# Cross-attention and ternary feed-forward on one core: the stores of keys and values issued from ScalarE's queue

## The reference, cut to what matters

```python
x = x + xattn(layernorm(x), ctx, ctx)      # x: 4 x 2048 x 512, ctx: 4 x 154 x 512
x = x + ffn(layernorm(x))

def xattn(q, k, v):                        # 16 heads of 32, 8 of keys and values
    q1, q2 = split(q @ Wq.T); k1, k2 = split(k @ Wk.T); v = v @ Wv.T
    w = softmax(q1 k1) - lam * softmax(q2 k2)
    return (rmsnorm(w @ v) * g * 0.2...) @ Wo.T

def ffn(x):
    scale = 1 / mean(abs(w))               # one for w1 (2048 x 512), one for w2
    wq = clip(round(w * scale), -1, 1) / scale
    h = gelu(layernorm(x) @ wq1.T + b1)
    return layernorm(h) @ wq2.T + b2
```

## Time and profile before

| | |
|---|---|
| median of 3 runs | 2423.88 us (2423.76 to 2427.24) |
| the profiled execution | 2423.49 us, its span 2421.5 us |
| PE busy | 2286.6 us, 94% |
| DVE, ACT, POOL busy | 71%, 55%, 41% |
| mean granted clock of PE | 0.983 |
| the prologue, until the first scores (PE L1344) | 163.5 us |

### The profile page before, as it was taken

How to read it: one execution, slowest core, us unless ns; L and a number is a source line. 1 busy time by engine, 2 the same in 40 slices (tenths; PEclk the granted TensorE clock), 3 DMA queues, 4 the chain that set the end, 5 groups by cost and what they waited for, 6 DMA issues and landing times.

```text
span 2421.5 us, 35774 instructions
## 1 busy us (share of the span) xinstructions
PE 2286.6 (94%) x13791; PEld 1083.1 (45%) x13791; DVE 1714.2 (71%) x2701; ACT 1339.7 (55%) x1945; POOL 993.4 (41%) x807
## 2 busy tenths in 40 slices
PE   8679999999999999999989999999999999999978
PEld 5344534445353544535344454534445453544433
DVE  4677768686785868678676867868676786867663
ACT  3435655556465555656555555655556565555544
POOL 0102625436172534627153452715346271534517
PEclk9779999999999999999999999999999999999989
DMA  7412103030210303021130302112040211203000
GB/s 262 120 25 62 27 24 83 15 92 15 78 30 29 78 15 92 15 66 27 43 79 15 92 15 66 28 47 59 15 107 15 66 28 50 56 15 75 15 22 18
DMA packets 105661, 125.88 MB, mean 52 GB/s; under 512 B 22512, under 2 KB 74284, under 8 KB 104980
## 3 DMA queue, kind: packets, MB, share of 16 engines
q1 hardware_dynamic: 105492, 123.60, 18.4%
HBM read 51.80 MB, written 20.36 MB: 30 GB/s over the span
## 4 chain that ended last, share of the span: by engine, by line
PE 70%; DVE 17%; DMA 3%; ACT 3%; POOL 3%; issue 3%; SPq 1%; POOLq 0%; ACTq 0%; DVEq 0%
PE ps L1421 16%; PE ps L1443 9%; PE ps L1433 9%; PE ps L1319 5%; PE ps L1366 5%; PE ps L1344 4%; PE ps L1264 4%; PE ps L1373 4%; PE ps L1265 3%; PE ps L1266 3%; DVE attn_raw L993 2%; DVE arena L1052 2%; DVE arena L941 2%; DMA arena<-in_x 2%; DVE arena L955 2%
## 5 line engine op out<-in xcount | busy, mean ns | idle before, releaser
L563 POOL TENSOR_TENSOR attn_raw<-attn_raw 128x512 f32<-128x512 f32 x448 | 579.1, 1311 | 153.5 <-ACT attn_raw L720 146.2
L1421 PE MATMUL ps<-rows,w1T 128*128 128x512 f16 x2048 | 486.9, 381 | 24.8 <-DVE rows L1047 24.8
L955 DVE TENSOR_REDUCE arena<-ps 128x3 f32<-128x462 f32 (+1 forms) x704 | 413.0, 618 | 111.0 <-PE ps L1319 110.1
L529 POOL TENSOR_TENSOR q<-q 128x512 f16<-128x512 f32 x128 | 158.3, 1241 | 723.3 <-ACT q L666 706.6
L715 ACT ACTIVATE attn_raw<-ps,vec_cols,wstep 128x512 f32<-128x512 f32 x256 | 198.7, 776 | 276.3 <-PE ps L1421 274.4
L1052 DVE SCALAR_TENSOR_TENSOR arena<-attn_raw,vec_cols,arena 128x512 f16<-128x512 f32 x256 | 231.8, 905 | 86.1 <-ACT arena L718 84.5
L1421 PEld LDWEIGHTS ps<-rows,w1T 128*128 128x128 f16 x2048 | 191.8, 98 | 222.1 <-DVE rows L1047 38.0
L1443 PE MATMUL ps<-w2T,arena 128*128 128x512 f16 x1088 | 271.2, 379 | 0.0
L686 ACT ACTIVATE arena<-ps 128x1024 f32<-128x1024 f32 x128 | 131.6, 1028 | 228.3 <-PE ps L1344 228.3
L975 DVE SCALAR_TENSOR_TENSOR p<-arena,p 128x512 f16<-128x512 f32 x128 | 88.1, 688 | 236.7 <-ACT p L690 236.7
L1319 PE MATMUL ps<-k_att,stack_raw 96*128 96x154 f16 x2048 | 222.0, 233 | 27.2 <-DVE arena L955 25.2
(11 more groups left out here) (183 smaller groups left out, 3478.7 us busy)
## 6 DMA issues: line engine op xcount, KB each, us to landing
stack_raw<-q SPq DMA_DIRECT2D x768, 64.0 KB, 2.0
arena<-in_x SPq DMA_DIRECT2D x64, 256.0 KB, 2.7
out<-arena SPq DMA_DIRECT2D x64, 256.0 KB, 2.1
arena<-in_x SPq DMA_DIRECT2D x15, 1024.0 KB, 6.2
arena<-in_L_ffn_w SPq DMA_DIRECT2D x7, 1024.0 KB, 10.1
stack_raw<-in_L_xattn_Wq SPq DMA_DIRECT2D x8, 256.0 KB, 5.8
k_att<-k_store SPq DMA_DIRECT2D x4, 490.0 KB
k_store<-attn_raw SPq DMA_DIRECT2D x12, 160.0 KB
```

Of the source, the lines that this page charges most:

```text
L563: ins = pool.tensor_tensor(acc[:, e, :], acc[:, e, :], src[:, j % NG, :], ALU.add)
L955: dve.tensor_reduce(negmax[:, tt, u0:u1], ps[:, row_bank(c, tb), 0:(u1 - u0) * S].rearrange("p (u s) -> p u s", s=S), AX.X, ALU.max, negat ...
L1421: ins = pe.matmul(ps[:, B_H + j % 2, :], w1T[:, k, j * P:(j + 1) * P], rows16[:, e, k, :], start=(k == 0 and e == 0), stop=(k == KD - 1 an ...
```

## The change

ACT issues the stores, each right behind the work of a tile: constant rows at tile 12, keys of m at tile 13 + m, values of b at tile 18 + b. The buffers of values 2 and 3 stand in `q32` and in half of `q16`; both are cleared at the start, and the memset and the wait ahead of batch 2 are gone. The first queries' copies wait for these two stores instead. Each value store has a semaphore of its own. The sums of pieces 6, 7 and 8 stand beside tiles 23, 24 and 25. The transposes of block 1 (x1) stand behind m7 on PE and behind m8 on DVE, ahead of the bias vector.

```diff
-                     "m6 t15 m7 m8 m9 m10 b0 x1 n0")
+                     "m6 t15 m7 x1 m8 m9 m10 b0 n0")
...
-DVE_PROLOGUE = tokens("x0 a0 ... m6 m7 m8 m9 m10 n0 b0 x1 n1")
+DVE_PROLOGUE = tokens("x0 a0 ... m6 m7 m8 x1 m9 m10 n0 b0 n1")
-ACT_PROLOGUE = tokens("x0 q0 q1 a0 q2 t0 t1 ...
+ACT_PROLOGUE = tokens("x0 q0 q1 q2 t0 t1 ...
...
-SUMS_BY_ACT, SUMS_BY_DVE = {17: 0, 19: 2, 20: 4, 22: 5, JH * 2: 7}, {18: 1, 20: 3, JH * 2: 6, JH * 2 + 1: 8}
+SUMS_BY_ACT, SUMS_BY_DVE = {17: 0, 19: 2, 20: 4, 22: 5, 24: 7}, {18: 1, 20: 3, 23: 6, 25: 8}
...
-        v_new = [attn_raw[:, at:at + 3 * TB // 2] for at in (6 * TB, 15 * TB // 2, 0, 3 * TB // 2)]
-        v_first, v_second = attn_raw[:, 6 * TB:], attn_raw[:, 0:3 * TB]
+        v_first = attn_raw[:, 6 * TB:]
+        v_new = [v_first[:, 0:3 * TB // 2], v_first[:, 3 * TB // 2:],
+                 q32[:].rearrange("p b t -> p (b t)")[:, 0:3 * TB // 2],
+                 q16[:, 1].rearrange("p a b t -> p (a b t)").bitcast(F32)[:, 0:3 * TB // 2]]
...
@@ block.sync, setup @@
-                    if n == N_KV_TILES:
-                        sp.wait_ge(s_krows, 2)
-                        for b in range(BATCH):
-                            sp.dma_start(k_store[STK:STKM, :, b, :], krows).then_inc(s_krst, 16)
-                    if 0 <= n - T_KEYS - NSTG < KUNITS // UPT:
-                        store_keys(n - T_KEYS - NSTG)
-                    b = n - T_VALUES - NSTG
-                    if 0 <= b < BATCH:
-                        sp.wait_ge(s_vnew, 9 * b + 9)
-                        sp.dma_start(v_store[b], v_new[b]).then_inc(s_vst[b % 2], 16)
...
@@ block.scalar, setup, at the end of a tile's work @@
+                    if n == T_KEYS:
+                        act.wait_ge(s_krows, 2)
+                        for b in range(BATCH):
+                            act.dma_start(k_store[STK:STKM, :, b, :], krows).then_inc(s_krst, 16)
+                    if 0 <= n - T_KEYS - 1 < KUNITS // UPT:
+                        store_keys(n - T_KEYS - 1)
+                    if 0 <= n - T_VALUES - 2 < BATCH:
+                        store_values(n - T_VALUES - 2)
                     if n in SUMS_BY_ACT:
                         weight_sum(n)
...
@@ block.scalar, q_hi @@
+                if c == 0 and n in (0, 2):
+                    act.wait_ge(s_vst[2 + n // 2], 16)
...
@@ block.vector @@
+                dve.memset(v_new[2], 0.0)
+                dve.memset(v_new[3], 0.0)
                 dve.memset(v_first, 0.0).then_inc(s_v0, 1)
...
-                        if b == 2:
-                            dve.wait_ge(s_kst, 16 * 3 * KUNITS // UPT)
-                            dve.memset(v_second, 0.0).then_inc(s_v0, 1)
-                            dve.wait_ge(s_v0, 2)
```

More of the change, by code:

```diff
@@ L79 @@
 PE_PROLOGUE = tokens("x0 q0 q1 a0 q2 t0 t1 t2 q3 t3 t4 t5 q4 t6 t7 m0 q5 t8 t9 m1 q6 t10 m2 t11 q7 m3 t12 m4 t13 m5 t14 "
-                     "m6 t15 m7 m8 m9 m10 b0 x1 n0")
-DVE_PROLOGUE = tokens("x0 a0 t0 t1 t2 t3 t4 t5 t6 t7 t8 m0 t9 t10 m1 t11 m2 t12 m3 t13 m4 t14 s1 m5 t15 r1 m6 m7 m8 m9 m10 "
-                      "n0 b0 x1 n1")
-ACT_PROLOGUE = tokens("x0 q0 q1 a0 q2 t0 t1 t2 q3 t3 t4 t5 q4 t6 t7 q5 t8 t9 q6 t10 t11 q7 t12 t13 t14 t15 x1")
+                     "m6 t15 m7 x1 m8 m9 m10 b0 n0")
+DVE_PROLOGUE = tokens("x0 a0 t0 t1 t2 t3 t4 t5 t6 t7 t8 m0 t9 t10 m1 t11 m2 t12 m3 t13 m4 t14 s1 m5 t15 r1 m6 m7 m8 x1 m9 m10 "
+                      "n0 b0 n1")
+ACT_PROLOGUE = tokens("x0 q0 q1 q2 t0 t1 t2 q3 t3 t4 t5 q4 t6 t7 q5 t8 t9 q6 t10 t11 q7 t12 t13 t14 t15 x1")
 POOL_PROLOGUE = tokens("q0 q1 q2 q3 q4 q5 q6 s1 q7")
@@ L273, in build @@
         s_kv, s_k_hi, s_k_lo = sem("kv_product"), sem("k_hi"), sem("k_lo")
-        s_kst, s_vst = sem("k_stored"), [sem("v_stored0"), sem("v_stored1")]
+        s_kst, s_vst = sem("k_stored"), [sem(f"v_stored{b}") for b in range(BATCH)]
         s_krst, s_vnew = sem("key_rows_stored"), sem("v_new")
@@ L376, in _ @@
         def _(sp):
[L377 to L383, removed]
             def setup():
@@ L399, in setup @@
                         sp.dma_start(dst, src).then_inc(s_w[piece], 16)
-                    if n == N_KV_TILES:
-                        sp.wait_ge(s_krows, 2)
-                        for b in range(BATCH):
-                            sp.dma_start(k_store[STK:STKM, :, b, :], krows).then_inc(s_krst, 16)
-                    if 0 <= n - T_KEYS - NSTG < KUNITS // UPT:
-                        store_keys(n - T_KEYS - NSTG)
-                    b = n - T_VALUES - NSTG
-                    if 0 <= b < BATCH:
-                        sp.wait_ge(s_vnew, 9 * b + 9)
-                        sp.dma_start(v_store[b], v_new[b]).then_inc(s_vst[b % 2], 16)
                 sp.wait_ge(s_krst, 16 * BATCH)
                 sp.wait_ge(s_kst, 16 * 3 * KUNITS // UPT)
-                for half in range(2):
-                    sp.wait_ge(s_vst[half], 16 * BATCH // 2)
+                for b in range(BATCH):
+                    sp.wait_ge(s_vst[b], 16)
                 load_keys(0)
@@ L605, in _, with store_keys, store_values @@
         def _(act):
+            def store_keys(m):
+                act.wait_ge(s_k_lo, 2 * m + 2)
+                for c3, e in enumerate((0, 0, 1)):
+                    dst = k_store[DH * c3:DH * c3 + DH, UPT * m:UPT * m + UPT, :, :]
+                    act.dma_start(dst.rearrange("d u b s -> u d (b s)"), k16[:, m, e, :, :].rearrange(
+                        "p b s -> p (b s)")).then_inc(s_kst, 16)
+            def store_values(b):
+                act.wait_ge(s_vnew, 9 * b + 9)
+                act.dma_start(v_store[b], v_new[b]).then_inc(s_vst[b], 16)
             def setup():
@@ L645, in weight_sum @@
                 abs_out = q16[:, 0].rearrange("p a b t -> p (a b t)")[:, 0:words]
-                if n not in range(len(tiles)):
-                    act.wait_ge(s_kst, 16 * 3 * KUNITS // UPT)
-                    abs_out = attn_raw[:, 4 * TB:6 * TB].bitcast(F16)
                 act.activation(abs_out, src, ACT.Abs, accum_out=wabs[:, w, col:col + 1]).then_inc(s_aabs, 1)
@@ L761, in _ @@
                     ternary_copy(n)
-                elif what == "a":
-                    weight_sum(JH * 2)
                 elif what == "x":
@@ L855, in weight_scales @@
             def weight_scales():
-                for n in (JH * 2, JH * 2 + 1):
-                    weight_sum(n)
                 dve.tensor_copy(b1ln16[:, :, 0], b1ln_col).then_inc(s_b1ln, 1)
@@ L883, in ternary @@
                 pair = sign_pair(n)
-                if n in (2, 4):
+                if n == 2:
                     for half in range(2):
-                        dve.wait_ge(s_vst[half], 16 * (n // 2))
+                        dve.wait_ge(s_vst[half], 16)
                 if 8 <= n < JH:
@@ L1236, in bias_vector @@
                 pe.wait_ge(s_ternC, JH)
-                wait(pe, s_q32, 0, QM, QM)
+                pe.wait_ge(s_xt_lo, 2 * TT)
                 pe.wait_ge(s_b1ln, 2)
@@ L1525, in _ @@
                     if n:
-                        pe.wait_ge(s_bias, 2)
+                        pe.wait_ge(s_ternC, JH)
+                        wait(pe, s_q32, 0, QM, QM)
                     x_transposes(n)
```

## The result

| | before | changed |
|---|---|---|
| median of 12 runs each, side by side | 2424.78 us (2420.71 to 2428.84) | 2429.53 us (2424.19 to 2433.77) |
| ratio | | 1.0018, 95% interval 1.001 to 1.0026 |
| span of the profiled execution, granted clock | 2421.5 us, 0.983 | 2427.8 us, 0.979 |
| T, `woT_lo` of tile 16 begins | 42.39 | 59.09 |
| X, x0 ready | 87.2 | 94.3 |

The change is 4.75 us slower by the medians, 0.18 to 0.2%. That is small, but the interval lies above 1. The page's first line answers to the earlier trace rows; only PE's busy time has grown, by 4.9 us for the same number of matmuls, with a mean granted clock of 0.979 in place of 0.983.

The account below looks back on a forecast made before the run. With PE 94% busy and the loop untouched, the prologue before the first scores was taken to decide: -8.0 (start included), -4.5 and +0.4 make -12.1, plus 13.1 for ACT's queue gives +1.0 on 2423.49: 2424.5 us, range 2411 to 2430.

Parts of the forecast that it names:

- the case that I called likeliest: Prologue: ACT's queue pays back what the prologue gains; 2421 to 2428 us, chance 0.43.
- the slower rival: Prologue: a cold PE behind a late ACT, T 57 or later; 2428.9 to 2431 us, chance 0.22.
- The start: Start of the kernel: two added memsets ahead of DVE's release of the constants, +1.4 us.
- T to X without the wait: Prologue, tile 16's `woT_lo` to x0 ready: 35.3 us instead of 44.8, wait and memset gone, two sums added.
- The stores on ACT's queue: Prologue: key stores hold ACT about as they held SyncE, T 13.1 us late at 56.9; +13.
- X to m0: Prologue, x0 ready to m0: totals no longer wait for sums and PE keeps its clock; -4.5 us.
- x1: Late prologue: m8 2.0 us later, DVE 2.7 more ahead of m9, 4.3 saved before the maxima's copy; +0.4.
- quick stores: ACT's queue: ACT gets its stores away quickly, T below 51; 2411.4 to 2414.3 us, chance 0.35.
- Cold PE: Prologue: T 57 or later, PE at 1.2 GHz makes values 3 late by 4.4 us; 2428.9 to 2431, chance 0.22.

Follow-up runs that it names:

- e7: Changed kernel with the two added memsets (values 2 and 3) on GpSimd instead of DVE: 2426.91 us, ratio 1.0008 to the kernel before.
- e1: Changed kernel with the key store laid out so that a store leads with 128 rows instead of 4 x 32: 2412.37 us, ratio 0.9961 to the kernel before.
- e14: Changed kernel with all stores issued by GpSimd, block 0's rstd behind the second group: 2413.06 us, ratio 0.9958 to the kernel before.
- e5: Changed kernel with block 1's transposes alone put back behind the bias vector: 2428.61 us, ratio 1.0018 to the kernel before.
- e2: Kernel before with the 128-row layout of the key store, all stores on SyncE's queue: 2411.26 us, ratio 0.9954 to the kernel before.
- e11: As e10, but GpSimd takes the last eighth of the first queries ahead of block 1's rstd: 2411.91 us, ratio 0.9947 to the kernel before.
- e10: As e2, with only the sums of pieces 6, 7 and 8 moved as in the change: 2411.10 us, ratio 0.9945 to the kernel before.
- e3: Changed kernel with all stores back in SyncE's queue, old 4 x 32 layout: 2418.87 us, ratio 0.9984 to the kernel before.
- e16: Changed kernel with 128-row layout, added memsets on GpSimd, block 1's rstd late, stores issued by GpSimd: 2410.23 us, ratio 0.9941 to the kernel before.
- e17: Changed kernel with 128-row layout, added memsets on GpSimd, block 1's rstd late, stores issued by SyncE: 2412.09 us, ratio 0.9949 to the kernel before.
- e4: Kernel before with only the key stores and constant rows moved to ACT's queue: 2427.12 us, ratio 1.0013 to the kernel before.
- e12: Changed kernel with 128-row layout, added memsets on GpSimd, block 1's rstd late, stores on ACT: 2412.59 us, ratio 0.9955 to the kernel before.

## Why the prediction was right, and where its steps were off

The forecast was no change, +1.0, with a range of 2411 to 2430. The measured median, 2429.53, lies inside it by 0.5 us. It is outside the 2421 to 2428 of the case that I called likeliest, and in the stretch that the slower rival had opened for a reason that did not come true. So that the range holds it is in part luck. The mechanism of the likeliest case did come true: what the prologue gains is paid back in ACT's queue. By its steps:

- **The start**: 1.4 predicted; DVE's big memset begins 1.6 us later (5.75 against 4.14), and e7 gives 1.7 of T back without the added memsets. Right.
- **T to X without the wait**: 35.4 predicted, 35.2 measured in the changed kernel, in e1 and in e14. Right.
- **The stores on ACT's queue**: T at 56.9 predicted, 59.1 measured, so +15.3 over 43.8 instead of +13.1. The choice of the high end was right: stores on four engines held ACT as they had held SyncE. The sizes were not: I gave the second group SyncE's 6.22 us, and it took 13.9, while the first took 4.8 for 6.74. T came only 2.2 us later than predicted because the second group began at 38.4, where my sum had it at 42.4, and ACT's work ahead of the third, 1.98 in the sum, took 0.3: two errors the other way covered 5.7 of these 7.6 us. In SyncE's queue a store waits behind the weights and then has the four engines alone; in ACT's it goes beside them, about packet for packet. The Trainium skill's "DMA: Bandwidth & Descriptors", section "Queues, rings and completion order", has this turn, and the counts above agree with it; what I read out of it, half for the stores, was half of the packets and a quarter of the time.
- **X to m0**: -4.5 predicted, 113.48 - 94.33 = 19.2 instead of 22.0, so -2.8. After the queue's this is the term that was furthest off. The totals did follow the second query, but I took PE's clock as kept, and the first eight of the first query's matmuls ran 0.43 us apart, at 1.2 GHz, in place of 0.22. In e5 they ran at full clock and m0 was at X + 17.5 on PE, as predicted. Against e2, the moved sums cost 2.1 us ahead of x0 and saved 4.1 behind it in e11, at full clock, and 2.4 in e10, where the half clock came with them.
- **x1**: +0.4 predicted, up to the copy of the maxima. m8 came 1.7 later against m0 and 2.4 were saved behind it, so -0.7; against e5 0.3 of the gain was left at block 0's second round of scores.

Up to the copy of the maxima this makes 7.1 - 2.8 - 0.7 = +3.6 (162.69 against 159.05) where the prediction had +1.0: 2.2 more from the queue, 0.2 less from T to X, 1.7 more from X to m0, 1.1 less from x1. The rest, about 1 us of the median, is not resolved.

One reading of mine was too strong: I set the 3.63 us of a store against a DMA share of 0.27. That store was issued from 39.87 to 43.50, and the share was 1.06 at 40 to 41, 0.44 at 41 to 42 and 0.30 at 42 to 43: the engines were full at first, and only the end of the issue shows the four alone.

Of the rivals, **quick stores** had T below 51 as its mark, and it was 59.1; e1 and e14 are what that rival would have been, 2412.4 and 2413.1, inside its 2411.4 to 2414.3. The price was right, and the condition, that a queue of its own gives four-engine stores the way, did not hold for ACT's queue. The Trainium skill's section "Issuing engines are not separate DMA queues" of the same page calls the time to issue "usually small relative to the DMA itself": 0.33 to 1.05 us a store in e1, with a median of 0.46, agree with it, 6.50 us in the changed kernel do not. The same page's section "Why a DMA increments its semaphore by 16 and not by 1" lets the slowest dimension set the number of engines, and for ACT's queue the runs agree: with 4 in the pattern 4.2 engines are busy, and with 128 the stores move at 3.7 times the rate beside the weights. **Cold PE** had its first half: with T over 57, PE stood and the first of values' products ran at half clock:

```profile
66.03 3.78 PE L1197 MATMUL ps<-stack_raw 128*128 128x256 f32 x8 [11.87 <-DVE attn_raw L846]
```

but the next took 2.23 and then 1.9, so DVE never waited for values 3 (X = T + 35.2). Its 2428.9 to 2431 holds the measured median, for another reason: a longer hold in ACT's queue, and the half clock at the first query.

## What to carry to other kernels

Before a store is moved to another engine's queue to free the first, look at its issue time beside the DMA share. Here a store took up to 3.6 us to issue, and the last microsecond of each such issue passed with 0.27 to 0.30 of the DMA in use, after a full start; the pattern, with 4 as its outer size, was the bound, and the hold moved with the stores to whatever stood behind them on ACT. Mend the pattern first (here one rearrangement, 11 to 12 us), then the queue hardly matters. Where the pattern can't be mended, an engine that has nothing else to do is the one to issue from; e14 supports this, though GpSimd's queue also spread the stores more widely. And an early edge in the prologue need not reach the end of a kernel whose PE is at 94%: in e11 3.8 us at the first scores were nothing in the time.

## What the hardware showed that I had not expected

- ACT's stores and SyncE's loads took turns on the DMA engines at about one packet for one, whatever the packets' sizes: 55 ns of the one against 84 or 311 ns of the other (256 packets against 259 in e1; 70 against an estimated 62 on four engines in the changed kernel).
- The same store pattern, 4 x 32 x 640, went over four DMA engines in packets of 1280 B when SyncE or ACT issued it, and in packets of 5120 B, up to 13 at once, when GpSimd did.
- The very same code, x0's copies followed by the first query, ran at 2.4 GHz in the profiles of before, e2, e3, e5, e11, e16 and e17; in those of the changed kernel, e1, e4, e7, e10, e12 and e14 the query's first seven to ten matmuls ran at 1.2 GHz, at a price of about 1.6 us. The programs of e10 and e11 do not differ ahead of it. What decides it stays open.
